# Moving the weighted values of a group of attention heads through DRAM

## The reference

```python
scores = jnp.einsum('bkgqd,bkmd->bkgqm', qg, k) / np.sqrt(HEAD_DIM)
scores = jnp.where(causal, scores, -jnp.inf)
attn = jax.nn.softmax(scores, axis=-1)
out = jnp.einsum('bkgqm,bkmd->bkgqd', attn, v)
out = out.transpose(0, 2, 1, 3).reshape(b, s, HIDDEN)
return out @ Wo
```

## Time and profile before

| | us |
|---|---|
| timed, median of 3 | 2409.13 (2407.0 to 2411.66) |
| the profiled execution | 2416.49 |
| its span | 2414.8 |
| PE busy | 2254.6 (93%) |
| DVE / ACT / POOL busy | 1464.6 / 1183.2 / 506.3 |
| mean granted TensorE clock | 0.963 |

### The profile page before, as it was taken

One profiled execution on the slowest core, in us unless ns is written; L12 is line 12 of the kernel. 1 busy time (PEld: TensorE's weight loads), 2 busy tenths in 40 slices (PEclk: granted clock), 3 DMA queues, 4 the chain that ended last, 5 costly groups with the idle time before them and its releaser, 6 DMA issues.

```text
span 2414.8 us, 36047 instructions
## 1 busy us (share of the span) xinstructions
PE 2254.6 (93%) x12664; PEld 1220.6 (51%) x12664; DVE 1464.6 (61%) x3257; ACT 1183.2 (49%) x2273; POOL 506.3 (21%) x646
## 2 busy tenths in 40 slices
PE   6688898999999999999899999989898999999998
PEld 5455554545455455555555555545443444444443
DVE  6767787857667576787877778777752221221222
ACT  5465677645556465565666666576861101011010
POOL 4433323212312122131312222122220000000000
PEclk8699898999999999999999999999999999999999
DMA  5000324312313123231413133243323000000000
GB/s 179 1 1 19 104 82 164 103 47 72 117 42 114 35 58 120 80 108 53 144 53 112 54 106 116 78 122 98 100 61 97 0 18 0 14 5 5 13 1 18
DMA packets 135122, 163.59 MB, mean 68 GB/s; under 512 B 41616, under 2 KB 96912, under 8 KB 134672
## 3 DMA queue, kind: packets, MB, share of 16 engines
q1 hardware_dynamic: 134944, 161.29, 21.7%
HBM read 94.51 MB, written 53.35 MB: 61 GB/s over the span
## 4 chain that ended last, share of the span: by engine, by line
PE 76%; DMA 6%; DVE 6%; ACT 4%; SPq 3%; issue 2%; POOL 1%; ACTq 0%; POOLq 0%; DVEq 0%
PE ps L1505 15%; PE ps L1443 10%; PE ps L1516 7%; PE ps L1413 7%; PE ps L1397 7%; PE ps L1422 5%; PE ps L1458 5%; PE ps L1367 3%; PE ps L1286 3%; DMA scr_q<-big 3%; PE ps L1372 3%; PE ps L1467 2%; PE ps L1490 2%; PE ps L1378 1%; DVE peaks L2086 1%
## 5 line engine op out<-in xcount | busy, mean ns | idle before, releaser
L2086 DVE TENSOR_REDUCE peaks<-ps 128x4 f32<-128x512 f32 x960 | 625.0, 681 | 220.3 <-PE ps L1367 91.3
L1697 ACT ACTIVATE big<-ps 128x512 f32<-128x512 f32 x960 | 551.5, 603 | 362.7 <-PE ps L1397 252.9
L1901 POOL TENSOR_SCALAR_AFFINE_SELECT big<-big 128x512 f32<-128x512 f32 x384 | 248.3, 660 | 1010.6 <-ACT big L1697 1010.2
L1505 PE MATMUL ps<-xt,big 128*128 128x512 f32 x896 | 390.1, 593 | 2.8 <-issue 2.8
L1397 PE MATMUL ps<-big 99*128 99x512 bf16 (+3 forms) x1536 | 347.5, 305 | 23.5 <-ACT big L1697 18.2
L1443 PE MATMUL ps<-big,xt 128*128 128x512 f32 (+1 forms) x768 | 295.7, 497 | 0.5 <-DVE peaks L2086 0.2
L1505 PEld LDWEIGHTS ps<-xt,big 128*128 128x128 f32 x896 | 168.8, 190 | 209.3 <-issue 208.2
L1413 PE MATMUL ps<-big,vs 128*32 128x512 f32 (+3 forms) x3072 | 247.7, 450 | 11.5 <-POOL big L1901 8.2
L1786 ACT ACTIVATE t<-ps 128x512 f32<-128x512 f32 x56 | 33.5, 598 | 457.6 <-PE ps L1505 457.6
L1686 ACT ACTIVATE ps<-cbf 128x512 f32<-128x512 bf16 x384 | 230.8, 605 | 37.3 <-DVE peaks L2086 31.5
L2142 DVE SCALAR_TENSOR_TENSOR t<-rest,t 128x512 f32<-128x512 f32 x56 | 38.7, 691 | 280.4 <-PE ps L1505 276.8
(11 more groups left out here) (225 smaller groups left out, 2906.2 us busy)
## 6 DMA issues: line engine op xcount, KB each, us to landing
big<-scr_q SPq DMA_DIRECT2D x96, 384.0 KB, 4.1
scr_q<-big SPq DMA_DIRECT2D x48, 384.0 KB, 2.9
scr_q<-big SPq DMA_DIRECT2D x48, 256.0 KB, 3.1
recb<-scr_sums SPq DMA_DIRECT2D x96, 128.0 KB
big<-scr_k SPq DMA_DIRECT2D x48, 192.0 KB, 3.3
big<-in_ffn_gu SPq DMA_DIRECT2D x14, 512.0 KB, 6.2
scr_q<-big SPq DMA_DIRECT2D x48, 128.0 KB, 3.2
ctxt<-ots SPq DMA_DIRECT2D x192, 32.0 KB
```

The source lines that it names most:

```text
L1505: mm = pe.matmul(bank_of(kind, n, m), wgu[:, m // 2, c, way, m % 2 * P:(m % 2 + 1) * P], xt[:, c, :], start=(c == 0), stop=(c == DC - 1))
L1697: act.activation(probs[:, i * S:(i + 1) * S], bank_of("exp", g, i), ACT.Exp, scale=1.0 / 16 if attn_of(n) == 1 else 0.25).then_inc(made["p ...
L1901: pool.affine_select(block_, block_, [[0, GQ], [1, P]], ALU.is_ge, zero, base=0, channel_multiplier=-1).then_inc(made["cut"], 1)
L2086: dve.tensor_reduce(to, blocks, AX.X, ALU.max, negate=True).then_inc(made["negmax"], 1)
```

## The change

The five small DMAs inside SBUF (four of values, one of sums) become one DMA of all of `ots` to a DRAM tensor `scr_heads`, and two DMAs back: the four rows of sums to `sums`, and the 64 rows of values to `heads`. SyncE waits for the first to land before it issues the other two. `ots` may be overwritten once `heads_out` has counted; the reciprocal waits for both of the DMAs that come back, which share the semaphore `moved`. The planner gets a new part `heads_out` (600 ns, landing 2000 ns), and `nums` is now 800 ns instead of 2500.

```diff
     if kind == "pack":
-        return [("SP", "nums", k, 2500), ("DVE", "rec", k, 330), ("SP", "recs", k, 700), ("SP", "recb", k, 700)] + scaled
+        return [("SP", "heads_out", k, 600), ("SP", "nums", k, 800), ("DVE", "rec", k, 330), ("SP", "recs", k, 700), ("SP", "recb", k, 700)] + scaled
...
     if name == "ot":
-        return [("pv_full", (n, 1))] + ([("nums", (n - 1,))] if n else [])
+        return [("pv_full", (n, 1))] + ([("heads_out", (n - 1,))] if n else [])
+    if name == "heads_out":
+        return [("ot", k)] + ([("nums", (n - 1,))] if n else [])
     if name == "nums":
         free = heads_free(n // 8) if n % 8 == 0 else None
-        return [("ot", k)] + ([free] if free else []) + ([("recs", (n - 1,))] if n else [])
+        return [("heads_out", k)] + ([free] if free else []) + ([("recs", (n - 1,))] if n else [])
...
+        scr_heads = nc.dram_tensor("scr_heads", (P, S), F32).ap()
...
+            def heads_to_dram(g):
+                sp.wait_ge(made["ot"], counted("ot", g))
+                if g:
+                    sp.wait_ge(moved, 32 * g)
+                sp.dma_start(scr_heads, ots[:]).then_inc(heads_out, 16)
+
             def move_heads(g):
 
                 n, c = g // 8, g % 8 // 2
-                sp.wait_ge(made["ot"], counted("ot", g))
+                sp.wait_ge(heads_out, 16 * (g + 1))
...
                 at = GQ * HD * (g % 2)
-                for h in range(GQ):
-                    sp.dma_start(heads[n % 2][at + h * HD:at + (h + 1) * HD, c, :], ots[32 * h:32 * h + HD, :]).then_inc(moved, 16)
-                sp.dma_start(sums[:], ots[HD:P:32, :]).then_inc(moved, 16)
+                rows = scr_heads.rearrange("(h w) t -> h w t", h=GQ)
+                sp.dma_start(sums[:], rows[:, HD, :].rearrange("h (b t) -> h b t", t=HD)).then_inc(moved, 16)
+                sp.dma_start(heads[n % 2][at:at + GQ * HD, c, :], rows[:, 0:HD, :]).then_inc(moved, 16)
...
             def out_heads(g):
                 act.wait_ge(made["pv_full"], counted("pv_full", g, 1))
                 if g:
-                    act.wait_ge(moved, 80 * g)
+                    act.wait_ge(heads_out, 16 * g)
...
             def invert(g):
-                dve.wait_ge(moved, 80 * (g + 1))
+                dve.wait_ge(moved, 32 * (g + 1))
```

More of the change, by code:

```diff
@@ L326, in pieces @@
     return [("SP", kind, k, 700 * (3 if kind == "load_experts" else 1))]
-LANDS = {"load_ffn1": 8000, "cw": 2300, "shift_out": 2000, "shift_in": 2000, "keys": 3000, "queries": 3400, "nums": 2300, "recs": 2000, "recb": 2300, "load_proj": 6200,
+LANDS = {"load_ffn1": 8000, "cw": 2300, "shift_out": 2000, "shift_in": 2000, "keys": 3000, "queries": 3400, "heads_out": 2000, "nums": 2300, "recs": 2000, "recb": 2300, "load_proj": 6200,
          "load_dense": 5000, "load_rope": 4000, "load_experts": 8000, "load_down": 9000,
@@ L933, in program @@
         queries_in = [flat_sem(f"queries_in{k}") for k in range(6)]
-        moved, recs_out, recb_in = flat_sem("moved"), flat_sem("recs_out"), flat_sem("recb_in")
+        heads_out, moved = flat_sem("heads_out"), flat_sem("moved")
+        recs_out, recb_in = flat_sem("recs_out"), flat_sem("recb_in")
         shift_out = flat_sem("shift_out")
@@ L1220, in flow_loads @@
                         shift_rows(*k)
+                    elif kind == "heads_out":
+                        heads_to_dram(*k)
                     elif kind == "nums":
@@ L2112, in scale_heads @@
                 dve.wait_ge(recb_in, 16 * (8 * n + 2 * c + 2))
-                dve.wait_ge(moved, 80 * (8 * n + 2 * c + 2))
+                dve.wait_ge(moved, 32 * (8 * n + 2 * c + 2))
                 dve.tensor_tensor(heads[n % 2][:, c, :], heads[n % 2][:, c, :], recb[:], ALU.mult).then_inc(made["ctn"], 1)
```

## The result

| | before | after |
|---|---|---|
| median of 4 runs | 2408.65 us | **2487.95 us** |
| least to most | 2407.0 to 2411.66 | 2483.18 to 2494.95 |
| ratio, 95% interval | | 1.033 (1.0303 to 1.0357) |
| span of the profiled execution | 2414.8 us | 2481.5 us |
| granted clock of TensorE, mean | 0.963 | 0.956 |

The change costs 79 us. The sign was forecast, but 12 us were expected, and 2487.95 lies far above the range of 2403 to 2438.

A forecast was written before the change was run, and what follows sets the result against it. The prediction took TensorE, busy 93% of 2414.8 us, as the bound. Its terms 6 + 2 + 2.5 + 3.2 - 2 gave +12 us on the 2409.1 us median: 2421 us, range 2403 to 2438.

The forecast's parts named there:

- The last group: Before the last output projection of attention: values land 2.2 to 4.1 us later with nothing to cover it, +3.2 us.
- the longer hole adds no second fall: In the last group's hole, the granted clock already falls, so lengthening it costs no further clock.
- A group's lateness: From the write of `ots` to the last landing in each group: 6.2 us against 4.4, 1.8 us later.
- I take a tenth: Share of 67 us of new vector-engine waits at the reciprocal that reaches TensorE: +6 us (0 to 12).
- SyncE comes out even, and nothing shown makes it the bound: On SyncE, 134 us of issue spared against 83 us of waits for the write and its 0.35 us issues.
- The relief of -2: At 10 of 12 batches, chunk writes leave SyncE about 2.1 us earlier: a gain of 2 us.
- The rival in which SyncE is relieved: SyncE was the bound at batch boundaries; a quarter of TensorE's 68.5 idle us goes: 2395 us, chance 0.17.
- Less one maximum: On the vector engine, the planner puts the reciprocal behind 61 more maxima over 96 groups, sheltering 0.43 us per group.
- Two landings in a row at every boundary: At 12 batches the write, then the sums, queue behind chunk writes; 25 us more, 2446 us, chance 0.10.
- (a): At 1443 us, chunks written and weights loaded at once: landing 1 to 4.2 us later, +2 us.
- (b): At 1505 us, behind a load of weights: landing 1.7 to 4.2 us later, +2.5 us.
- Everything but the end is hidden: Rival: only the loss before the last output projection remains, mostly cancelled by SyncE's relief: 2410 us, chance 0.26.

The follow-up runs named there:

- experiment 2: After's three DMAs through DRAM, all issued at the one old step, with before's planner and order: 2513.58 us, ratio 1.044.
- experiment 7: Before plus one idle write of `ots` to DRAM per group, on which SyncE waits only for the write before last: 2415.42 us, ratio 1.0029.
- 10: Before plus an idle write of `ots` per group, with SyncE standing until that write has landed: 2449.38 us, ratio 1.0156.
- 5: After's DMAs in before's order, with sums and values on semaphores of their own: 2469.28 us, ratio 1.027.
- 12: Before's order, values through DRAM, sums by one small DMA inside SBUF right behind the write, on their own semaphore: 2439.97 us, ratio 1.0132.
- 3: After, with the sums on a semaphore of their own, so the reciprocal waits for the sums alone: 2450.15 us, ratio 1.0187.
- 6: Before, with two more unused 128x512 reductions on the vector engine behind each reciprocal, no DMA changed: 2434.32 us, ratio 1.0123.
- 4: After, with the planner told that the reads land after 4600 ns instead of 2300: 2453.73 us, ratio 1.018.
- 1: After's planner order, with before's five small DMAs inside SBUF issued where the two reads stood: 2429.38 us, ratio 1.0086.

## Why the prediction was wrong, point by point

**The whole of it, in before's order.** Four steps between measured kernels make up the 106 us of experiment 2: the bytes 7 (experiment 7), SyncE standing until they have landed 31 (10 less 7), the sums' longer way through DRAM 27 (5 less 10; by 12 it is 33), and the reciprocal's wait for the slow read of the values 41 (2 less 5). After's order gives back 27. Each step is a difference of kernels with intervals of 4 to 10 us to either side, and the four add up to 106 by the way they are formed, which proves nothing; in 10 the write stands behind the small DMAs, in 5 ahead of the reads, so the two middle terms are sizes, not exact shares. In after's own order only one split was measured: 21 for the order with its later issue, 58 for the DMAs, of which 34 go with the semaphore.

**Right.** The reciprocal's waits grow, and SyncE waits for the write. The four-block read is slow. ScalarE's waits before it overwrites `ots` are as before, 81.6 us in 80 (79.9 in 73). The bytes cost little. The last group, here in the chain of after:

```profile
1895.27 7.95 DMA scr_heads<-ots
...
1903.23 0.57 SPq L1202
...
1903.86 3.83 DMA big<-scr_heads
...
1907.72 0.26 DVE sums L2120
...
1909.41 3.70 DMA recb<-scr_sums
```

From ScalarE's last copy into `ots` to the end of the program it is 590.3 us before and 593.8 after: +3.5, where +3.2 was said. By the trace the last of the data lands 20.0 us after that copy against 15.9, so 4.1 us later, at the upper end of the prediction's 2.2 to 4.1. But TensorE's wait there grew only from 8.2 to 8.7 us, not to 11.5:

```profile
PE ps L1434 <- DVE big L2126: 8.7, 1, 8.7
```

The reason is the granted clock, by stretch. The first two lines are of before: 7 us from 2 us behind the start of ScalarE's last copy on, and 10.5 us from the middle of the hole on. The other two are the same places in after:

```profile
1826.00:1833.00 7.00, 6.35 (x15) 2.96 (x16) 0.00 (x0) 1.08 (x2) 0.00 (x0) 1.00 1.06 346
...
1842.00:1852.50 10.50, 6.24 (x8) 2.66 (x9) 0.69 (x1) 0.00 (x0) 0.00 (x0) 0.51 0.04 14
...
1889.00:1896.00 7.00, 6.05 (x8) 2.54 (x9) 0.00 (x0) 0.00 (x0) 0.00 (x0) 0.51 1.05 342
...
1909.50:1920.00 10.50, 6.12 (x8) 2.58 (x9) 0.69 (x1) 0.00 (x0) 0.00 (x0) 0.51 0.05 14
```

In the hole itself the clock is the same in both, 0.51 over 10.5 us, that is at the lower level; so "the longer hole adds no second fall" held. What is new lies ahead of the hole: for 7 us TensorE was granted 0.51 where it had 1.00. It ran out of work 17.5 us after the copy instead of 13.5, and 7 us at half speed account for 3.5 of these 4. That kept the wait short, but not the path to the end. Why the clock fell there is open: in the 20 us ahead TensorE was busy 17.6 us against 17.4 in before, where it did not fall.

**A group's lateness: too small.** The prediction had 6.2 us from the write to the last landing against 4.4, 1.8 us later. From the end of ScalarE's copy into `ots` to the last landing, the means over the 96 groups are 8.15 against 5.0 us, 3.15 later. The reads were off by little (4.6 us from the issue of the sums, 4.1 said). The write lands after 2.09 us in the median as said, but after 2.87 on average: in 16 of the 96 groups it takes 4 to 9.6 us, most of them where chunks are written or weights loaded. A median of quiet places was used for a sum over all of them. The slack was averaged in the same way: 0.65 us were taken off in all 96 groups, though in 24 of them the vector engine already stood waiting and had none. With 24 x (1.8 - 0.43) + 72 x (1.8 - 0.65 - 0.43) the prediction's own numbers give 85 us, not 67 (an estimate). The vector engine's new waits before the last group came to 135.3 - 38.7 = 97 us. SyncE's wait for the write is about 160 us, not the 80 of the list of signs:

```profile
SPq L1202 <- DMA scr_heads<-ots: 159.4, 86, 9.2
```

**"I take a tenth": the step that failed.** Removing 102 us of these waits gave back 34 us, a third (3); in before's order 160 us gave 41, a quarter (5); work added to the vector engine costs 0.24 to 0.30 of itself (6). In 3 and 5 SyncE's wait for the reciprocal fell as well, by 93 us (3) and from 225.1 to 114.0 us (2 to 5), so the price there is that of both engines together; 6, where SyncE's waits hardly changed, has the vector engine alone. The tenth leaned on two quiet stretches of the earlier trace rows in which TensorE lost nothing. Those were probably places where the planner had put cover for a wait that it knew of. It plans the landing at 2.3 us, and with 4.6 told (4) 36 of the 79 us are gone. With a third, 97 us would have made 32 and not 6, and the whole sum 38 us instead of 12; the rest of the 79 lies in the next steps.

**"SyncE comes out even, and nothing shown makes it the bound": the second.** Its issue time was balanced against its waits, as if they cost alike. But no run shows that SyncE needed the issue time saved, and the wait stands ahead of the shift's and the factors' DMAs. Standing alone costs 31 us (10), and an idle write without it 7. The relief of -2 wasn't seen anywhere. The rival in which SyncE is relieved, with a chance of 0.17, fell entirely.

**"Less one maximum": the order.** The order's change was counted as a shelter of 0.43 us per group. With the old DMAs in it, it costs 21 us (1). Why is not settled: the maxima are later for ScalarE (51.4 against 31.5 us), and the DMAs are issued 1.0 us later on average.

**The rivals.** "Two landings in a row at every boundary" (chance 0.10, 2446 us) is the nearest and is real. It expected some 25 us of lost TensorE time at the boundaries, and the twelve intervals with the chunk writes have 26.5 us more idle time than before; the chain at 1470 us shows one of them. The forecast had priced only two such places, (a) and (b), at 4.5 us. But the other intervals lost as much again, 24.3 us, and the clock took 16 us, so this rival alone does not give 79 either. "Everything but the end is hidden" fell with nearly every term of the sum but the last group's.

## What to carry to other kernels

In this kernel a wait of the vector engine came through to TensorE at a quarter to a third of itself, and not at a tenth. What the share is elsewhere takes a run; a stretch in which nothing was lost proves only that this wait was covered. And sum over the full places, not from the median of the quiet ones: half of the added idle time came in one interval in eight. When DMAs are joined, look at which landing each waiter needs and at what else the joined one holds: here three DMAs in place of five put a full landing, and SyncE's standing for it, ahead of the 8 KB that the path needed. Give each waiter a semaphore of its own and issue first what is waited for first: it adds no DMA, and it was the only thing that beat the kernel before (by 6 us, 1 to 10).

## What the runs showed of the hardware that was not expected

- Many small DMAs inside SBUF were cheaper than few large ones through DRAM. Five, of 32 KB and 8 KB, are all in 4.43 us after ScalarE's copy (median); write, wait and two reads take 7.07. The Trainium skill, page "DMA: Bandwidth & Descriptors", section "Rules for kernel authors", would join them, as transfers below 64 KB are mostly overhead. Here the issue time saved bought nothing that a run shows, and the second landing stood on the path.
- A write of 256 KB lands after 2.1 us in a quiet queue and after 9.22 us behind loads and chunk writes (1470 us), with the same bytes; a wait for it is priced by what was issued ahead of it.
- Around a hole of 7.6 us TensorE's granted clock fell, and it was 0.74 from 1485.5 to 1500 us, that is, at the lower of its two levels for about half of these 14.5 us. In this profile the loss shows twice, as 51 us of idle time and as 16 us of slower matmuls.
- The clock also fell ahead of a hole, with TensorE busy 17.6 of the 20 us before (0.51 from 1889 to 1896 us), where the kernel before kept 1.00 at the same place with 17.4 us.
